# Two accumulators by turns for the dense sums, one bank for both kinds of placings, four or five banks for the builds of layer 1

## The reference

```
xn  = layernorm(x)
gnn: s = h @ W; msg = s[src] * edge_weight; out = segment_sum(msg, dst)   # twice: W1, then W2
x   = x + gnn(gnn(xn)) + mix(xn)          # mix: linear attention, k and v normed by head, kv = sum over all rows
x   = x + ffn(layernorm(x))               # 16 experts, the best 2 of each row, then a layernorm
```

## Time and profile before

| | us |
|---|---|
| median of 3 runs | 3532.04 (3525.42 to 3533.8) |
| profiled execution | 3563.73 |
| its span, first to last instruction | 3561.7 |
| layer 1, from its first plane to the first plane of layer 2 | 1303.6 |
| layer 2, to the end of its last plane | 1222.2 |
| all before and behind | 127 + 908.9 |

### The profile page before, as it was taken

The page is one execution under the profiler, slowest core; times in us unless marked ns, Lnnn a source line. Parts: engine busy times, 40 slices in busy tenths (PEclk is TensorE's granted clock), DMA queues, the critical chain, the costliest instruction groups (busy, mean ns, idle before and its releaser), DMA issues.

```text
span 3561.7 us, 48771 instructions
## 1 busy us (share of the span) xinstructions
PE 2840.4 (80%) x14412; PEld 2015.7 (57%) x14413; DVE 1395.8 (39%) x3855; ACT 1370.9 (38%) x2993; POOL 1922.7 (54%) x2019
## 2 busy tenths in 40 slices
PE   1799999999999999788778787888877648999930
PEld 0466556566566656555555555555556647888820
DVE  8455545455554554322222222222225641111157
ACT  4687767777777773000000000000004423333322
POOL 2555555566565564466666666666643551222235
PEclk9999999999999999888888888989888868999975
DMA  6344344344444436655555555555532334444454
GB/s 217 118 154 155 115 151 156 117 160 157 145 131 155 155 120 199 197 161 161 160 158 167 161 163 158 164 156 164 162 106 84 116 123 132 139 145 133 125 156 122
DMA packets 268415, 527.04 MB, mean 148 GB/s; under 512 B 58823, under 2 KB 155086, under 8 KB 268096
## 3 DMA queue, kind: packets, MB, share of 16 engines
q0 software_dynamic: 88848, 240.99, 22.3%
q1 hardware_dynamic: 148256, 252.66, 21.7%
q10 hardware_dynamic: 31120, 31.04, 2.7%
HBM read 394.15 MB, written 131.79 MB: 148 GB/s over the span
## 4 chain that ended last, share of the span: by engine, by line
PE 54%; another core or an unknown queue 15%; issue 11%; DVE 7%; ACT 5%; DMA 4%; SPq 2%; ACTq 0%; DVEq 0%; POOL 0%; POOLq 0%
PE bank L994 23%; PE bank L982 12%; PE sums L1008 5%; PE bank L1217 4%; DMA pa<-ys_d 3%; PE bank L1205 2%; PE bank L1018 1%; PE bank L1078 1%; ACT build L795 1%; ACT build L793 1%; PE sums L965 1%; PE bank L1027 1%; PE bank L1144 1%; ACT pa L916 1%
## 5 line engine op out<-in xcount | busy, mean ns | idle before, releaser
L688 POOL DMA_INDIRECT pa<-xn_d,srcs x816 | 783.5, 960 | 537.7 <-PE sums L1008 321.5
L994 PE MATMUL bank<-t1s,pa 128*128 128x256 f32 x2450 | 643.4, 414 | 153.9 <-ACT ob L818 83.3
L688 POOL DMA_INDIRECT pa<-h_d,srcs x544 | 528.4, 971 | 307.2 <-issue 150.3
L994 PEld LDWEIGHTS bank<-t1s,pa 128*128 128x128 f32 x2450 | 497.3, 209 | 281.9 <-issue 121.5
L982 PE MATMUL bank<-build 128*128 128x343 f32 x1500 | 514.9, 484 | 138.8 <-DVE build L1376 60.9
L994 PE MATMUL bank<-t0s,pa 128*128 128x256 f32 x2450 | 558.7, 384 | 9.8 <-DVE pa L1394 8.0
L1394 DVE TENSOR_TENSOR pa<-bank,pa 128x343 f32 x750 | 378.0, 514 | 422.0 <-PE bank L982 183.7
L994 PEld LDWEIGHTS bank<-t0s,pa 128*128 128x128 f32 x2450 | 461.3, 191 | 108.6 <-issue 48.0
L982 PEld LDWEIGHTS bank<-build 128*128 128x128 f32 x1500 | 276.5, 197 | 350.0 <-issue 278.6
L795 ACT ACTIVATE build<-build,ones 128x343 f32<-128x343 f32 x750 | 436.3, 582 | 24.4
L793 ACT ACTIVATE build<-build,tabs 128x343 f32<-128x343 f32 x750 | 424.9, 567 | 41.1 <-issue 27.4
(11 more groups left out here) (257 smaller groups left out, 2716.2 us busy)
## 6 DMA issues: line engine op xcount, KB each, us to landing
slab_d<-pa SPq DMA_DIRECT2D x175, 448.0 KB
pa<-slab_d SPq DMA_DIRECT2D x175, 448.0 KB
pa<-in_w ACTq DMA_DIRECT2D x32, 512.0 KB, 3.9
pa<-in_w SPq DMA_DIRECT2D x32, 512.0 KB, 3.6
pa<-ys_d SPq DMA_DIRECT2D x109, 130.0 KB
pa<-xn_d,srcs POOLq DMA_INDIRECT x816
pa<-eo_d SPq DMA_DIRECT2D x49, 256.0 KB, 3.1
pa<-h_d,srcs POOLq DMA_INDIRECT x544
```

The costliest lines, as they stand in the source:

```text
L688: pool.indirect_dma_start(gath2[b * QT + j], None, table, bass.IndirectOffsetOnAxis(ap=srcs[:, n:n + 1], axis=0)).then_inc(s_g[b], 16)
L994: ins = pe.matmul(app[:, 0:D], slab3[:, s, :], table[:, s * D:(s + 1) * D], start=s == 0, stop=s == T - 1)
```

## The change

Bank 7 becomes a second accumulator: even units sum in bank 4 and odd ones in bank 7, and plane 0 of a unit waits for the copy of the unit before the last one. Both kinds of placings go into bank 6 (`plc`), so each placing waits until every placing before it has been added, of both kinds. The builds of a unit use banks 2, 3, 5 and the accumulator that this unit will use; once the dense placing stands behind them, the other accumulator joins, so 4 banks become 5. A table (`build_at`) says for every build which bank it takes and which add it waits for.

The dense placing is moved. `free_for_dense` looks for the first place at which no placing of the other kind is near. In layer 1 that is build 5 in 16 units, 12 in 4 and 19 in 4 (before: 2), with DVE's add 4 chunks later instead of at plane 0. In layer 2 it is plane 1 in 12 units and 2, 3 and 4 in 4 units each (before: 1), with the add a plane later and ahead of that plane's other work. The work itself, its shapes and its count, is the same.

```
-        bld, app, plg, pld = [bank[2], bank[3], bank[5]], bank[4], bank[6], bank[7]
+        app, plc = [bank[4], bank[7]], bank[6]
+        def free_for_dense(i, layer, where, last, behind):
+            for at in range(last[0], last[1]):
+                so_far = STEPS * i // NU if not layer else STEPS * max(i - 1, 0) // (NU - 1)
+                near = []
+                for n in range(KB if where == "m" else CT):
+                    for s in steps_at(i, where, n, layer):
+                        if n < at:
+                            so_far = s + 1
+                        if at - behind <= n < at + behind:
+                            near.append(s % QK)
+                if (so_far - 1) % QK != 1 and 1 not in near and 2 not in near:
+                    return at
+        dense_at = [[None] + [free_for_dense(i, layer, "mp"[layer], ((5, 24), (1, 6))[layer], (4, 1)[layer])
+                              for i in range(1, NU)] for layer in range(2)]
+        def build_banks(i):
+            banks, last, use, wait = [2, 3, 5, (4, 7)[i % 2]], {}, [], []
+            for m in range(KB):
+                if i > 0 and m == dense_at[0][i] + 1:
+                    banks.append((7, 4)[i % 2])
+                b = min(banks, key=lambda b: last.get(b, -1))
+                use.append(b)
+                wait.append(last.get(b, -1) + 1)
+                last[b] = m
+            return use, wait
...
-                pe.wait_ge(s_bev, c + 1)
-                pe.matmul(bld[c % BLD][:, 0:WT], lohot[c % LR], mvs[c % MR], start=True, stop=True
+                wait_from(pe, s_bev, i * KB + wait[m])
+                pe.matmul(bank[use[m]][:, 0:WT], lohot[c % LR], mvs[c % MR], start=True, stop=True
...
-                if p == 0 and d > 0:
-                    pe.wait_ge(s_obd, d)
+                if p == 0:
+                    wait_from(pe, s_obd, d - 1 if i > 0 else d)
...
-                wait_from(pe, s_pad, d)
+                wait_from(pe, s_pag, placed[0])
+                wait_from(pe, s_pad, placed[1])
...
-                    if m == 2 and i > 0:
+                    if m == dense_at[0][i]:
                         place_dense(i - 1, 0)
...
-                    if p == 1 and i > 0:
+                    if p == dense_at[1][i]:
                         place_dense(i - 1, 1)
...
+                    if i > 0 and m == dense_at[0][i] + 4:
+                        place_add(1, GU + i - 1, t1s)
                     add_chunk(i, m, at)
...
-                    if p == 0 and i > 0:
-                        place_add(1, GU + i - 1, t1s)
...
+                    if i > 0 and p == dense_at[1][i] + 1:
+                        place_add(1, GU + i - 1, t0s)
                     all_gathered(steps_at(i, "p", p, 1), 1, t0s)
-                    if p == 2 and i > 0:
-                        place_add(1, GU + i - 1, t0s)
```

More of the change, by code:

```diff
@@ L431, in ring_of @@
             return s % size, used + s // size, size
+        def free_for_dense(i, layer, where, last, behind):
[10 more added lines that the diff above has]
+                    return at
+            assert False
+        dense_at = [[None] + [free_for_dense(i, layer, "mp"[layer], ((5, 24), (1, 6))[layer], (4, 1)[layer])
[10 more added lines that the diff above has]
+            return use, wait
+        build_at = [build_banks(i) for i in range(NU)]
         def chunk_at(m):
@@ L817, in take_dense @@
                 act.nop(nofuse=True)
[L818 removed]
+                act.activation(ob[1][:], app[i % 2][:, 0:D], ACT.Copy).then_inc(s_obd, 1)
             act.wait_ge(s_pool, 8)
@@ L993, in apply @@
                 for s in range(p * CT, (p + 1) * CT):
-                    ins = pe.matmul(app[:, 0:D], slab3[:, s, :], table[:, s * D:(s + 1) * D], start=s == 0,
+                    ins = pe.matmul(app[i % 2][:, 0:D], slab3[:, s, :], table[:, s * D:(s + 1) * D], start=s == 0,
                                     stop=s == T - 1)
@@ L1015, in place_gathered @@
                 pe.wait_ge(s_hpg, 2 * g + 2)
-                wait_from(pe, s_pag, g)
+                wait_from(pe, s_pag, placed[0])
+                wait_from(pe, s_pad, placed[1])
+                placed[0] += 1
                 for h in range(2):
-                    ins = pe.matmul(plg[:, h * D:(h + 1) * D], hotp[0][h][:], ob[0][:], start=True, stop=True)
+                    ins = pe.matmul(plc[:, h * D:(h + 1) * D], hotp[0][h][:], ob[0][:], start=True, stop=True)
                 ins.then_inc(s_plg, 1)
@@ L1024, in place_dense @@
                 pe.wait_ge(s_hpd, 2 * d + 2)
-                wait_from(pe, s_pad, d)
+                wait_from(pe, s_pag, placed[0])
+                wait_from(pe, s_pad, placed[1])
+                placed[1] += 1
                 for h in range(2):
-                    ins = pe.matmul(pld[:, h * D:(h + 1) * D], hotp[1][h][:], ob[1][:], start=True, stop=True)
+                    ins = pe.matmul(plc[:, h * D:(h + 1) * D], hotp[1][h][:], ob[1][:], start=True, stop=True)
                 ins.then_inc(s_pld, 1)
@@ L1391, in add_chunk @@
                 dve.wait_ge(s_bmm, c + 1 + CREDIT)
-                dve.wait_ge(s_bev, c + BLD - (0 if i == NU - 1 else 1))
+                wait_from(dve, s_bev, c if i == NU - 1 else c - 1)
                 part = slab3[:, :, bass.ds(at[chunk_at(m)], W)]
-                dve.tensor_tensor(part, bld[c % BLD][:, 0:WT].rearrange("p (s w) -> p s w", w=W), part, ALU.add
+                dve.tensor_tensor(part, bank[build_at[i][0][m]][:, 0:WT].rearrange("p (s w) -> p s w", w=W), part, ALU.add
                                   ).then_inc(s_bev, 1)
```

15 lines of the change are left out of this document (8 added, 7 removed).

## The result

The changed kernel takes 3523.95 us (median, 3512.14 to 3540.79) against 3536.37 us for the kernel before (3525.42 to 3551.8): a ratio of 0.9967, with a 95% interval from 0.9954 to 0.9981. The forecast was 3433 us. The gain is 12 us, not 99.

A forecast was written before the change was run, and what follows sets the result against it. PE's order was taken to set the time, with layer 2 losing most. From the median of 3532 us, -83 - 35 - 17 + 6 + 30 = -99 us gave 3433 us, with a range of 3370 to 3516 us.

The forecast's parts named there:

- Layer 2, the waits, -83: Layer 2, plane 0: PE's 83.3 us of waits for ACT's copy of the sum all go, -83 us.
- Layer 2, the clock, -35: Layer 2 unit starts: PE's clock there rises towards that of the rest, -35 us, bounds 0 and 147.
- What is given back, +30, at most 118: Layer 2: PE, now faster, sometimes waits for gathered rows or at the placing, +30 us, bounds 0 and 118.
- rival B: Layer 2: POOL becomes the bound, all 168 us of its waits for PE are had, 3347 us in all; chance 0.07.
- The gap without releaser: Layer 2: PE's two large waits without a named releaser, 69.0 and 41.9 us, are not touched by the change.
- Layer 1, -17: Layer 1 builds: most waits for DVE's adds and the placing's 6.0 us wait go, -17 us, between 0 and 57.
- The shared bank, +6: Placings of both kinds: each also waits for the other kind's add, +6 us, in layer 2's closest pairs.
- DVE in layer 2, 0: Layer 2, plane 3: DVE waits for a late placing and delays the next edge matrices, 0 us, at most 8 units x 4 us.
- A: Layer 2: PE's late signals make it stop a plane later instead; 20 us gained, none in layer 1, 3512 us; chance 0.15.
- page's case: Whole kernel: the change makes no measurable difference; chance of same 0.06, shared with the rest of A.

The follow-up runs named there:

- one_acc_l2_d: Changed kernel with one accumulator again in layer 2, plane 0 waiting for the copy of the unit just done: 3527.98 us against 3532.84 before, ratio 0.9978.
- the second pair: Changed kernel unaltered and the kernel before, run and traced again in one set: 3516.9 us against 3537.97, ratio 0.9942.
- speed A: Sets of runs in which the kernel before the change took 3533 to 3578 us.
- speed B: Sets of runs in which the kernel before the change took 3245 to 3248 us.

## Why the prediction was wrong, step by step

- *Layer 2, the waits, -83.* The wait went, as forecast. Its time did not. This is the step that failed, and it failed in its first sentence: that PE's order sets the time, so that a wait of PE is time of the kernel. In its place the runs showed a layer that keeps 1.44 to 1.47 us for each gather, whether PE waits 71 us for the copy or not at all, and whether it has 72 us less to do or not. With the wait put back (`one_acc_l2_d`) the units don't get longer. The 9 us at most that layer 2 gained are those of its first unit. A copy made 49 us earlier is also 2.8 times the longest wait of 17.5 us, not four times; that changes nothing here.
- *Layer 2, the clock, -35.* In the later units it stayed at 0.89 (0.88 and 0.87 in the second pair). I tied the low clock to the standstills at unit starts. The runs fit PE's idle time as a whole better: with less work it fell from 0.87 to 0.85, with fewer gathers, where the standstills without releaser fell to 40 us, it rose to 0.99.
- *What is given back, +30, at most 118.* All of 83 + 35 less 9 was. I had read POOL's 168.5 us of waits for PE as room that POOL has. In fact they were half of the evidence: PE stood 136 us without a releaser, while POOL stood 168 us for PE, in the same layer. If one engine is the bound, the other waits for it, but the bound does not stand still. At speed A neither set the pace by its own work. At speed B POOL did, as rival B had it, and layer 2 took 1055 to 1057 us, near the 1222 - 168 = 1054 us of that rival. With the earlier trace rows I could have divided: 1222.2 / 816 = 1.50 us for a gather, though POOL's own pace is 1.25, and no wait of PE named the gathers.
- *The gap without releaser.* I left the 69.0 and 41.9 us aside, since "nothing in the change touches them". They were part of the time in which PE was held to the pace. They rose from 136 to 183 us in all, and the busy time of PE by 23 us, and so took up 70 of the 83 us that the named wait set free; the layer as a whole got 9 us shorter.
- *Layer 1, -17.* Measured 22 us in this pair of traces and 16 us in the second, where the whole gain by the medians was 12 and 21 us. That the size is near is luck. The builds' waits for adds, to be under 5 us, were 15.7 us, and plane 0's rose from 8.0 to 36.7 us. Of the waits that were to go only the placing's 6.0 us went, and the 37.1 us without releaser, which I had left out, fell to 16.3 us.
- *The shared bank, +6; DVE in layer 2, 0.* No such cost is seen: placings waited 1.2 us for an add in layer 1, and no such wait is in the rows of layer 2. DVE did wait there for PE's placing ahead of the next matrix, 42 us in all, but no wait of PE for that matrix is in the rows.
- *Rivals.* A came nearest: PE's signals are late, not ACT's work, and the hold-up moves. It was nearest on the time (3512 us) and right on ACT's wait of 9.34 us, but it thought the late signals would meet another wait. They need none. The "page's case" of the chances is a sentence of the Trainium skill ("TensorE: Matmul & The Clock Gate", HAM oscillation): "Adding PSUM double-buffering gave no further gain". The page says it of a matmul kernel whose loop had first been rearranged so that PE stays warm, not of one whose PE waits in every turn. The outcome in layer 2 is like it (1135.0 against 1127.4 us), but the cause here is the pace of the gathers, which that sentence doesn't name.

What stays open is what makes a gather take 1.44 to 1.47 us at speed A. The runs exclude PE's work, the hand-over, POOL's own time, and the rows and bytes of the gathers. They leave something that goes by the number of gathers, or of their signals, and that delays PE's signals as well. No run tells gathers and signals apart, none at speed A leaves out the loads of the slab or alters the depth of the ring, and none tells whether the recording of the profile takes part: in the traces of the changed kernel it holds 548 of PE's 584 signals of layer 2 at speed A, and all 583 at speed B.

## What to carry to other kernels

A wait with a name on the busiest engine is worth its length only if that engine sets the pace. Before costing it, divide the stretch by the count of each kind of repeated work, and look whether another engine waits for the busy one at the same time. Where both stand still, as here (136 and 168 us), something else may set the pace, and time taken from one engine then comes back as standstill or half clock. An experiment that leaves out some of the busy engine's work, here 72 us, shows that in one run.

## What the hardware showed that I had not expected

- The same kernel runs at 3537 or at 3247 us, by set. Behind layer 2 the two agree (909.9 us in the trace of the changed kernel at speed A, 3244.6 - 2335.9 = 908.7 us at speed B); the two layers with the gathers make 267 of the 284 us between the two traces, and the time ahead of layer 1 the rest. The change is worth 0.3 to 0.6% at speed A and nothing at speed B.
- At speed A signals arrive late and together. So few signals of the slab's stores, and of the 816 gathers, are recorded there that the profile gives no time from issue to landing for them. The first row is of speed A, the second of B, where the last figure is that time, 5.7 us:

```profile
slab_d<-pa SPq DMA_DIRECT2D x175, 448.0 KB
```

```profile
slab_d<-pa SPq DMA_DIRECT2D x175, 448.0 KB, 5.7
```

- A step of PE whose rows have been requested stood 23 us behind the last gather of the step at speed A and 4 us at speed B (medians over 204 steps). At A 4 or 5 of the ring's 6 steps had been requested and not yet used when PE began a step.
